# Score pairs in runs of four, and value products of 512 queries, in a fused attention and mixture-of-experts kernel

## The reference

```python
q = apply_rope((x @ Wq.T + bq).reshape(B, T, H, D))      # B=4, T=1024, H=16, D=16
k = apply_rope((x @ Wk.T + bk).reshape(B, T, H, D))
v = (x @ Wv.T + bv).reshape(B, T, H, D)
scores = jnp.einsum('bthd,bshd->bhts', q, k) / np.sqrt(D)
attn = jax.nn.softmax(scores, axis=-1)
out = jnp.einsum('bhts,bshd->bthd', attn, v).reshape(B, T, C)
return out @ Wo.T + bo
```

## Time and profile before

| | |
|---|---|
| median of three runs | 1595.5 us |
| fastest and slowest of them | 1579.87 us, 1595.71 us |
| span of the profiled execution | 1571.8 us |
| what the median has beyond that span | 23.7 us |
| what the fastest run has beyond that span | 8.1 us |
| attention's scores, first to last | 142.7 to 791.2 us of the span |
| busy in the span: PE, DVE, ACT, POOL | 1435.0, 1110.0, 846.7, 431.5 us |

### The profile page before, as it was taken

How to read it: one execution, slowest core, us unless ns; L and a number is a source line. 1 busy time by engine, 2 the same in 40 slices (tenths; PEclk the granted TensorE clock), 3 DMA queues, 4 the chain that set the end, 5 groups by cost and what they waited for, 6 DMA issues and landing times.

```text
span 1571.8 us, 29999 instructions
## 1 busy us (share of the span) xinstructions
PE 1435.0 (91%) x9435; PEld 792.5 (50%) x9436; DVE 1110.0 (71%) x1983; ACT 846.7 (54%) x1613; POOL 431.5 (27%) x417
## 2 busy tenths in 40 slices
PE   7899999999999999999999259999999999999950
PEld 5454333333333333333355136777777777777740
DVE  6989999999999999997037764555545555555425
ACT  4523888888888888887856322222222222222215
POOL 5750000000000010001024143444444444444425
PEclk9999999999999999999999659999999999999985
DMA  6986364334636454640458804222221222222236
GB/s 205 263 222 116 77 170 97 60 73 75 100 57 123 65 90 65 102 70 26 148 90 205 281 25 96 33 30 33 33 33 31 33 33 31 33 33 33 32 88 197
DMA packets 125116, 141.80 MB, mean 90 GB/s; under 512 B 55131, under 2 KB 98949, under 8 KB 125030
## 3 DMA queue, kind: packets, MB, share of 16 engines
q1 hardware_dynamic: 109126, 121.98, 33.7%
q0 software_dynamic: 15904, 18.66, 7.5%
HBM read 86.30 MB, written 54.30 MB: 89 GB/s over the span
## 4 chain that ended last, share of the span: by engine, by line
PE 79%; DVE 7%; issue 5%; ACT 4%; POOL 2%; DMA 1%; SPq 1%; DVEq 0%; POOLq 0%; ACTq 0%
PE psum L1687 21%; PE psum L1525 17%; PE psum L1551 16%; PE psum L1706 12%; PE psum L1697 3%; PE psum L1618 2%; DVE mx L955 2%; PE psum L1537 2%; ACT work L1344 1%; PE psum L1616 1%; PE psum L1499 1%; ACT weights L1354 1%; PE psum L1485 1%; PE psum L1673 1%; PE psum L1637 1%
## 5 line engine op out<-in xcount | busy, mean ns | idle before, releaser
L955 DVE TENSOR_REDUCE mx<-psum 128x1 f32<-128x1024 f32 x512 | 621.8, 1222 | 19.1 <-PE psum L1525 16.7
L1344 ACT ACTIVATE work<-psum 128x512 f32<-128x512 f32 x1024 | 556.4, 597 | 80.6 <-PE psum L1537 18.1
L1525 PE MATMUL psum<-stack 48*128 48x512 f32 x1024 | 372.9, 445 | 6.6 <-DVE mx L955 6.1
L1537 PE MATMUL psum<-stack 50*128 50x512 f32 x1024 | 375.4, 446 | 0.0
L1687 PE MATMUL psum<-weights,values 128*128 x1136 | 341.1, 453 | 0.6 <-DVE values L1174 0.6
L1551 PE MATMUL psum<-work,values 128*32 128x256 f32 x4096 | 328.6, 393 | 9.2 <-ACT weights L1354 9.2
L1687 PEld LDWEIGHTS psum<-weights,values 128*128 128x128 f32 x1136 | 211.3, 191 | 99.6 <-issue 3.1
L1525 PEld LDWEIGHTS psum<-stack 48*128 48x128 f32 x1024 | 151.3, 185 | 217.1 <-DVE mx L955 183.6
L1421 ACT ACTIVATE values<-values 128x342 f32<-128x342 f32 x142 | 69.3, 488 | 250.5 <-DVE values L1186 250.5
L1706 PE MATMUL psum<-weights,work 114*128 (+1 forms) x852 | 198.6, 383 | 1.2 <-ACT work L1432 0.8
L1551 PEld LDWEIGHTS psum<-work,values 128*32 128x32 f32 x4096 | 82.2, 108 | 197.2 <-ACT work L1344 101.2
(11 more groups left out here) (184 smaller groups left out, 1185.4 us busy)
## 6 DMA issues: line engine op xcount, KB each, us to landing
stack<-qk_scr SPq DMA_DIRECT2D x192, 128.0 KB, 6.2
qk_scr<-weights SPq DMA_DIRECT2D x16, 1024.0 KB, 4.8
weights<-in_w SPq DMA_DIRECT2D x8, 1368.0 KB, 6.6
ot_scr<-weights SPq DMA_DIRECT2D x16, 512.0 KB, 3.2
weights<-in_w SPq DMA_DIRECT2D x8, 684.0 KB
work<-in_b SPq DMA_DIRECT2D x8, 684.0 KB, 8.8
y_d<-zeros SPq DMA_DIRECT2D x1, 4224.0 KB, 14.0
v_scr<-weights SPq DMA_DIRECT2D x32, 128.0 KB, 2.4
```

The source lines that it names most:

```text
L955: dve.tensor_reduce(mx[:, r, a, t:t + 1], bank(4 + 2 * a, 2), AX, ALU.max, negate=True).then_inc(s_max, 1)
L1344: act.activation(pt[u % 4][:, j, :], bank((c + HG * u + n) % 3), ACT.Exp, scale=SC).then_inc(s_exp, 1)
L1525: ins = pe.matmul(bank(4 + 2 * a + half), qs[t3][at:at + QROWS, r, P * t:P * (t + 1)], ks[t3][at:at + QROWS, r, 512 * half:512 * (half + 1 ...
L1537: pe.matmul(bank((t3 + HG * u + n) % 3), ks[t3][at:at + MROWS, r, P * st:P * (st + 1)], qs[t3][at:at + MROWS, r, 512 * half:512 * (half + ...
```

## The change

Before, each unit was two halves: two pairs, then value products of 256 queries for each of the four heads, then two pairs, then value products of the other 256 queries. After, all four pairs of a unit stand in a row, and behind them one value product of 512 queries for each head. The list `RUNS` gives pairs and queries of each run, for two units together. `cut` returns False everywhere, so that what it guards (a reduction of a first half) is never issued, and the two new semaphores are not used.

```diff
+RUNS = ((4, 512), (4, 512))
...
+def cut(m, a):
+
+
+    return False
...
-            def weigh(g, p, u, part):
+            def weigh(g, p, u, lo, hi):
 
                 half, st = u // ST, u % ST
-                if part == 0:
+                if lo == 0:
                     pe.wait_ge(s_exp, BLOCKS * g + HG * (u + 1))
...
-                at = 256 * part
                 for j in range(HG):
-                    last = pe.matmul(bank(3)[32 * j:32 * (j + 1), at:at + 256], vg[p][:, st, j, :],
-                                     pt[u % 4][:, j, at:at + 256], start=st + part == 0, stop=st + part == ST,
+                    last = pe.matmul(bank(3)[32 * j:32 * (j + 1), lo:hi], vg[p][:, st, j, :],
+                                     pt[u % 4][:, j, lo:hi], start=st == 0 and lo == 0, stop=st == ST - 1 and hi == 512,
                                      tile_position=(0, 32 * j))
-                if part == 1:
+                if hi == 512:
                     last.then_inc(s_pv, 1)
+
+            def weigh_two(g, p, u, lo, hi):
+
+                for n in range(2):
+                    first, last = max(lo - 512 * n, 0), min(hi - 512 * n, 512)
+                    if first < last:
+                        weigh(g, p, u + n, first, last)
...
-                for u in range(UNITS):
...
-                    for n in range(HG):
-                        if more:
-                            max_scores(g + ahead, (c + ahead) % 3, m, n // 2, n % 2)
-                        scores(g, t3, u, n)
-                        if n % 2 == 1:
-                            if u >= LAG:
-                                weigh(g, p, u - LAG, n // 2)
-                            elif c > 0:
-                                weigh(g - 1, 1 - p, UNITS + u - LAG, n // 2)
+                for u in range(0, UNITS, 2):
+                    pair, weighed = 0, 0
+                    for run, queries in RUNS:
+                        for q in range(pair, pair + run):
+                            v, n = u + q // HG, q % HG
...
+                                max_scores(g + ahead, (c + ahead) % 3, m, n // 2, n % 2)
+                            scores(g, t3, v, n)
+                        if u >= LAG:
+                            weigh_two(g, p, u - LAG, weighed, weighed + queries)
+                        elif c > 0:
+                            weigh_two(g - 1, 1 - p, UNITS + u - LAG, weighed, weighed + queries)
+                        pair, weighed = pair + run, weighed + queries
```

More of the change, by code:

```diff
@@ L83, in over, with cuts @@
     return (6 // m) * i + c // m
+def cut(m, a):
+    return False
+def cuts(m):
+    return sum(cut(n, 1) for n in range(m))
 def groups(eng, body):
@@ L432, in build @@
         s_mp = sem("max_scores_ready")
+        s_mq = sem("first_half_scores_ready")
+        s_mf = sem("first_half_max_done")
         s_max = sem("max_done")
@@ L951, in reduce_max @@
                 r, t = m // ST, m % ST
-                dve.wait_ge(s_mp, 2 * (UNITS * g + m) + a + 1)
+                unit, scored = UNITS * g + m, bank(4 + 2 * a, 2)
+                if cut(unit, a):
+                    dve.wait_ge(s_mq, cuts(unit) + 1)
+                    dve.tensor_reduce(scored[:, 511:512], scored[:, 0:512], AX, ALU.max).then_inc(s_mf, 1)
+                    scored = scored[:, 511:1024]
+                dve.wait_ge(s_mp, 2 * unit + a + 1)
+                if cut(unit, a):
+                    dve.wait_ge(s_mf, cuts(unit) + 1)
                 if t == 0 and a == 0:
                     after(dve, s_m2, PAIRS * (g - 1) + r + 1)
-                dve.tensor_reduce(mx[:, r, a, t:t + 1], bank(4 + 2 * a, 2), AX, ALU.max, negate=True).then_inc(s_max, 1)
+                dve.tensor_reduce(mx[:, r, a, t:t + 1], scored, AX, ALU.max, negate=True).then_inc(s_max, 1)
             def turn(g, r):
@@ L1528, in max_scores @@
                     ins.then_inc(s_mp, 1)
+                elif cut(UNITS * g + m, a):
+                    ins.then_inc(s_mq, 1)
             def scores(g, t3, u, n):
@@ new lines, in group @@
+                for u in range(0, UNITS, 2):
[3 more added lines that the diff above has]
+                            v, n = u + q // HG, q % HG
+                            ahead, m = 1 + (v + LEAD) // UNITS, (v + LEAD) % UNITS
+                            more = not (isinstance(g, int) and g + ahead >= NG)
+                            if more:
+                                if m == 0 and n == 0:
+                                    pe.wait_ge(s_stack[(c + ahead) % 3], STACK_DMAS * (over(i, c + ahead, 3) + 1))
+                                max_scores(g + ahead, (c + ahead) % 3, m, n // 2, n % 2)
[5 more added lines that the diff above has]
+                        pair, weighed = pair + run, weighed + queries
@@ L1599, in _ @@
             groups(pe, group)
-            for u in range(UNITS - LAG, UNITS):
-                for part in range(2):
-                    weigh(NG - 1, 1, u, part)
+            weigh_two(NG - 1, 1, UNITS - LAG, 0, 1024)
             pe.wait_ge(s_wo, 48)
```

4 lines of the change are left out of this document (removed).

## The result

The change makes the kernel slower. The median of four runs is 1638.27 us (1629.78 to 1642.92) against 1590.53 us for four runs of before (1579.87 to 1595.71). The ratio is 1.031, with a 95% interval of 1.026 to 1.036. The forecast was slower, by 1.7%, 1622 us; the measured median lies 1 us above the top of the range.

What follows compares the result with a forecast made beforehand. TensorE's list was taken as the bound at 2.46 us a unit; a loop of 2.60 adds 35.6 us, savings take off 9.3, so 26 us more: median from 1595.5 to 1622 us, range 1588 to 1637.

Steps and rivals of the forecast that it cites:

- The bound: In the body of attention before the change, TensorE's own list sets the pace at 2.46 us a unit; VectorE needs 2.26.
- The loop: In each unit the fourth score waits for the first one's exponential: 1.18 + 0.42 + 1.00 = 2.60 us, against 2.46.
- Rival 1: At the waiting fourth score, its weight load is hidden: 2.50 us a unit, no change, 1597 us; chance 0.20.
- Rival 2: At the fourth score, the bank comes within 0.9 us and VectorE's loop decides: 2.41 us a unit, 1573; chance 0.13.
- The save: Once in eight units, value products no longer wait for the output's saving; a late exponential costs 0.07 us instead of 0.37.
- The sum of the loop: Over attention, 254 units cost 35.6 us more and 31 savings 9.3 us less: 26 us more.
- the tail: In the units at the end without maxima, the loop is the same and they count among the 254 at 2.60 us.
- rival 3: Short TensorE waits in every unit bring its clock down some 3 us in each eight units: 40 us more, 1660; chance 0.07.
- The comparison: For the whole kernel, 26 us more takes the span from 1571.8 to 1598 and the median from 1595.5 to 1622 us.

Runs made afterwards that it cites:

- the tail in twos: The changed kernel with its last 20 units in the old order (two pairs, values of 256 queries); median 1604.95 us, ratio 1.005 to the kernel before.
- the unused products: The changed kernel with maximum products, read by nobody, issued also in the last 21 units; median 1608.05 us, ratio 1.011 to the kernel before.

## Why the prediction was right and where it was wrong

**The bound, right.** TensorE's list at 2.46 us a unit; VectorE not the bound.

**The loop, right to 0.02 us in the unit shown.** Product to exponential 0.53 (0.53 said), the fourth score 1.18 behind the first (1.18), the wait on the weight load and nothing of it hidden, so 0.43 to the values' load (0.42), 1.00 for the values (1.00), 2.62 us for this unit and 2.61 in the mean of attention's body (2.60). Shortening the exponential alone shortened the unit to 2.43, so the loop is shown and not only argued. Rival 1, the hidden load, would have given 2.50 and is refuted; with it the reading of the rule in the Trainium skill (TensorE: Matmul & The Clock Gate, "Step-by-step: what each phase is for") on loads pulled ahead, for a load that carries the wait: the load at 400.42 stands ahead of the product at 400.65, as the rule says, and the one that waits begins at 401.50 together with its product. Rival 2 needed a faster release and is refuted, though its own loop fits what was left at 2.43 (2.41 said) when the exponential was shortened.

**The save, right.** After, the first score at 402.94 of the trace has its exponential at 403.56, 0.09 later than elsewhere, and that unit is 0.08 longer (0.07 said); the wait of the values is gone (0.0 in the row of L1574 above).

**The sum of the loop, a little small.** 26 us; 29.7 measured with the clock held. By the sum a group is 16 x 0.14 - 2 x 0.30 = 1.64 us longer, by the traces 41.95 - 40.10 = 1.85, which makes 3.4 us over 16 groups: a hundredth of a microsecond in each unit.

**The step that failed: the tail, and with it rival 3.** The prediction says of the units at the end without maxima that "the loop is the same", and prices rival 3 as a fall in each eight units, with 0.07 for it and its time outside of the range. Its evidence was a clock of 1.00 over 565 us, all of it with maximum products beside the scores. Where they are missing the same wait leaves TensorE still for 0.45 us out of 2.60. The loop's length is indeed the same there (2.60 between 770 and 800 us), but the clock then falls, stays down through the rest of attention, and is down again in the output projection, a stage that the change doesn't touch. The sum put the clock at nothing. In the two profiled spans it is 30.1 - 1.3 = 29 us of the 60, of which the 14.7 of the projection are seen in this one trace; in ratios it is 2.6 points less the loop's 0.2 with the tail in twos, and 2.0 points with the unused products. It is not the same in each execution: group 15, at 40.5 with the clock held, took 44.7, 51.9 and 56.2 us in the three traces that have the fall. Why the clock holds for 22 to 43 us of such units before it falls stays open. Rival 3 was thus the right mechanism in the wrong place: not spread over attention, but in its last group and behind it.

**The comparison.** The sum was put on the median as if 23.7 us lay around a span. They don't, 1.8 do. The profiled execution of before was a fast one, 17 us below its median, and that of the changed kernel lies 4.6 below its own; so the medians differ by 47.7 us and not by the 60 of the two spans. What the clock does ahead of attention is one thing that differs between executions, by 18 us in the traces.

## What to carry to other kernels

Count the buffers against the longest run of producers, not against the mean: a run of four on three banks puts the whole way from product through consumer and back into every turn, even if the consumer's engine has time to spare on average, and what a saved switch is worth is small beside it. A wait that is added to the densest engine should be checked in each stage that it reaches, above all where that engine has the least to do beside it, and the stage behind belongs to the price: the clock can fall in one and be paid in the other. A helper engine's long step should stand behind the short one that others wait for; moving one here took 6 us out of the two groups in which it stood, and the ratio was 0.990 (0.984 to 0.997).

## What the runs showed of the hardware

- A weight load that carries a wait is exposed: the product behind it took 0.50 us instead of 0.39, and the values' load came 0.43 behind it instead of 0.32.
- Two value passes of 512 columns and four of 256 took the same 1.00 us with the way back.
- TensorE's clock stayed at its upper level with 0.45 us of idle in 2.60 us for 30 us and then fell (22 and 43 us in the two other traces with that tail); with extra products beside the scores, and the same waits, it stayed up. Once down, it stayed at half over 37 us, with TensorE busy 28.2 of 30 us.
- In the eight kernels in which GpSimd's multiplications were not moved, TensorE stops once each in groups 10 and 14, for 1.4 to 2.5 us. After fourteen of these sixteen stops the clock was at half for 3.4 to 20.5 us; after two it stayed up (1.51 us at 556 in the kernel before, 2.03 us at 751 with the unused products). With the stops removed, it was never at half from 180 to 820 us.
- A whole stretch of 75 to 85 us ahead of attention ran at half clock in some executions and not in others, in the old and in the new order. It costs 18 us.
